# Moving the unfolding of the image rows from VectorE to GpSimd in a Fourier-space MLP

## What is computed

```python
xf = jnp.fft.rfft2(x, axes=(1, 2), norm='ortho')             # B, H, W//2+1, 8 blocks, 96
xr, xi = (xf.real, xf.imag)
o1r = relu(einsum(xr, w1[0]) - einsum(xi, w1[1]) + b1[0])    # 'bhwni,nio->bhwno'
o1i = relu(einsum(xi, w1[0]) + einsum(xr, w1[1]) + b1[1])
o2r = einsum(o1r, w2[0]) - einsum(o1i, w2[1]) + b2[0]
o2i = einsum(o1i, w2[0]) + einsum(o1r, w2[1]) + b2[1]
xc = softshrink(stack([o2r, o2i]), 0.01)                     # as complex numbers
out = jnp.fft.irfft2(xc, s=(H, W), axes=(1, 2), norm='ortho') + x
```

## Time and profile before

| | |
|---|---|
| median of 3 runs | 5438.11 us |
| profiled execution, own time | 5438.1 us |
| its span, first to last instruction | 5436.3 us |
| TensorE busy | 5260.5 us, 97% |
| VectorE busy | 3214.6 us, 59% |
| ScalarE busy | 3140.4 us, 58% |
| GpSimd busy | 1254.0 us, 23% |
| HBM traffic | 78 GB/s over the span |
| mean granted TensorE clock | 0.991 |

### The profile page before, as it was taken

The page is one execution under the profiler, slowest core; times in us unless marked ns, Lnnn a source line. Parts: engine busy times, 40 slices in busy tenths (PEclk is TensorE's granted clock), DMA queues, the critical chain, the costliest instruction groups (busy, mean ns, idle before and its releaser), DMA issues.

```text
span 5436.3 us, 112618 instructions
## 1 busy us (share of the span) xinstructions
PE 5260.5 (97%) x42112; PEld 4947.7 (91%) x42112; DVE 3214.6 (59%) x5330; ACT 3140.4 (58%) x5680; POOL 1254.0 (23%) x810
## 2 busy tenths in 40 slices
PE   8999999999999999999999999999999999999997
PEld 8999989899898989999999999998999999999997
DVE  4666556565565665656656566565665556655565
ACT  6555566555665556655566555665556655566554
POOL 2211222112222022220222202222022220222200
PEclk9999999999999999999999999999999999999999
DMA  3331233321333213332133321334313333123312
GB/s 106 98 97 43 59 99 98 98 48 52 99 98 99 51 49 98 98 99 58 42 98 98 99 66 44 88 98 99 84 40 75 98 99 90 41 68 98 99 48 47
DMA packets 1131613, 430.06 MB, mean 79 GB/s; under 512 B 1130784, under 2 KB 1130912, under 8 KB 1131040
## 3 DMA queue, kind: packets, MB, share of 16 engines
q1 hardware_dynamic: 1131040, 422.23, 31.0%
HBM read 220.82 MB, written 201.33 MB: 78 GB/s over the span
## 4 chain that ended last, share of the span: by engine, by line
PE 95%; issue 2%; DVE 2%; ACT 1%; DMA 0%; DVEq 0%; SPq 0%; ACTq 0%
PE psum L563 17%; PE psum L604 14%; PE psum L578 13%; PE psum L653 13%; PE psum L627 13%; PE psum L637 8%; PE psum L590 7%; PE psum L665 4%; PE psum L666 3%; PE psum L667 3%; DVE x L529 1%; DVE mixed L498 1%; PE psum L622 0%; PE psum L645 0%; PE psum L644 0%
## 5 line engine op out<-in xcount | busy, mean ns | idle before, releaser
L498 DVE COPY mixed<-psum 128x768 f32<-128x768 f32 (+1 forms) x544 | 508.2, 934 | 1356.0 <-PE psum L590 1356.0
L332 POOL TENSOR_TENSOR doubled<-x 128x768 f32<-128x768 f32 x248 | 358.9, 1447 | 3883.0 <-DMA x<-x 3862.9
L563 PE MATMUL psum<-mats,x 128*96 128x128 f32 x8192 | 930.1, 277 | 63.9 <-issue 47.3
L563 PEld LDWEIGHTS psum<-mats,x 128*96 128x96 f32 x8192 | 918.2, 166 | 73.9 <-issue 53.8
L434 ACT ACTIVATE sums_high<-psum 128x512 fp32r<-128x512 f32 x768 | 459.9, 599 | 775.8 <-PE psum L653 775.8
L604 PEld LDWEIGHTS psum<-mats,mixed 128*128 128x128 f32 x6272 | 744.0, 191 | 121.1 <-issue 112.0
L604 PE MATMUL psum<-mats,mixed 128*128 128x128 f32 x6272 | 841.8, 283 | 0.0
L653 PE MATMUL psum<-mats,spectrum 128*128 128x128 f32 x6144 | 814.7, 278 | 26.4 <-DVE spectrum L505 26.4
L578 PE MATMUL psum<-w_whole,whole 128*128 128x192 f32 x4160 | 779.4, 329 | 55.7 <-ACT whole L365 47.0
L653 PEld LDWEIGHTS psum<-mats,spectrum 128*128 128x128 f32 x6144 | 756.9, 194 | 31.1 <-DVE spectrum L505 31.1
L627 PE MATMUL psum<-w2t,hidden 128*128 128x192 f32 x4160 | 768.4, 327 | 0.0
(11 more groups left out here) (69 smaller groups left out, 6403.6 us busy)
## 6 DMA issues: line engine op xcount, KB each, us to landing
x<-x SPq DMA_DIRECT2D x160, 768.0 KB, 7.3
out<-x SPq DMA_DIRECT2D x160, 768.0 KB, 8.2
x<-x SPq DMA_DIRECT2D x32, 1488.0 KB, 9.6
out<-x SPq DMA_DIRECT2D x32, 1488.0 KB, 10.6
x<-x SPq DMA_DIRECT2D x32, 816.0 KB, 4.9
out<-x SPq DMA_DIRECT2D x32, 816.0 KB, 4.6
w2t<-L_conv_w SPq DMA_DIRECT2D x128, 36.0 KB
w_halved<-L_conv_w SPq DMA_DIRECT2D x128, 24.0 KB
```

The lines of the kernel that those rows point to most:

```text
L498: dve.tensor_copy(mixed[s % 2][:, 0:k], both_b(s)[:, 0:k]).then_inc(b_copied, 1)
L563: last = pe.matmul(bank_a(at)[:, i * SIZE:(i + 1) * SIZE], xs[par][:, slot, :], mat(FW_EVEN if slot <= HALF else FW_ODD), start=True, stop ...
```

## The change

GpSimd does the unfolding for every unit. The three additions of the fold go into a helper, `halves` (the first two of them), which fold and a new `unfold` share; `unfold` waits for `f_added`, then makes the same 8 steps of 8 rows, each with three instructions, and counts `unfolded` 8 times a unit in place of 4. The rows 0 and 64 are not touched in it. GpSimd's program becomes: fold unit 1; then for each unit: unfold it, wait for that, fold the next unit of the same buffer, wait for that; at the end unfold the last two units. VectorE's loop over `PIECES` and the semaphore `unfold_even` are gone, so that VectorE goes from L529 straight to L468. A store waits for two counts of `unfolded` a piece.

```diff
@@ SyncE, store @@
-                    sp.wait_ge(unfolded, (m * 2 + par) * NP + (i + 1))
+                    sp.wait_ge(unfolded, (m * 2 + par) * NFOLD + 2 * (i + 1))
@@ GpSimd @@
+            def halves(t, i, done):
+                lo, hi = i * FOLD_ROWS + 1, min((i + 1) * FOLD_ROWS, HALF - 1)
+                up, down, twice = t[:, lo:hi + 1, :], mirrored(t, lo, hi), doubled[:, 0:hi + 1 - lo]
+                pool.tensor_tensor(twice, down, down, ALU.add).then_inc(pool_steps, 1)
+                pool.tensor_tensor(up, up, down, ALU.add).then_inc(pool_steps, 1)
+                return down, up, twice
...
+            def unfold(m, par, steps):
+                n = m * 2 + par
+                pool.wait_ge(f_added, n * NF + NF)
+                for i in range(NFOLD):
+                    if i > 0:
+                        pool.wait_ge(unfolded, n * NFOLD + i)
+                    down, up, twice = halves(xs[par], i, unfolded)
+                    pool.wait_ge(pool_steps, steps + 2 * (i + 1))
+                    pool.tensor_tensor(down, up, twice, ALU.subtract).then_inc(unfolded, 1)
...
-            fold(0, 1)
-            with pool.Fori(1, PAIRS) as m:
+            fold(0, 1, 0)
+            pool.wait_ge(x_folded[1], NFOLD)
+            with pool.Fori(0, PAIRS - 1) as m:
                 for par in range(2):
-                    pool.wait_ge(x_folded[1 - par], (m + par) * NFOLD)
-                    fold(m, par)
+                    steps = (1 + (m * 2 + par) * 2) * (2 * NFOLD)
+                    unfold(m, par, steps)
+                    pool.wait_ge(unfolded, (m * 2 + par + 1) * NFOLD)
+                    fold(m + 1, par, steps + 2 * NFOLD)
+                    pool.wait_ge(x_folded[par], (m + 2) * NFOLD)
+            for par in range(2):
+                unfold(PAIRS - 1, par, (1 + (PAIRS - 1) * 4 + par) * (2 * NFOLD))
+                pool.wait_ge(unfolded, ((PAIRS - 1) * 2 + par + 1) * NFOLD)
@@ VectorE, at the end of a unit @@
-                    dve.wait_ge(f_added, n * NF + NF)
-                    for i in range(NP + 1):
-                        if i < NP:
-                            lo, hi = PIECES[i]
-                            dve.tensor_tensor(x_unit[:, lo:hi + 1, :], x_unit[:, lo:hi + 1, :], mirrored(x_unit, lo, hi),
-                                              ALU.add).then_inc(unfold_even, 1)
-                        if i > 0:
-                            lo, hi = PIECES[i - 1]
-                            dve.wait_ge(unfold_even, n * NP + i)
-                            dve.scalar_tensor_tensor(mirrored(x_unit, lo, hi), mirrored(x_unit, lo, hi), -2.0,
-                                                     x_unit[:, lo:hi + 1, :], op0=ALU.mult,
-                                                     op1=ALU.add).then_inc(unfolded, 1)
```

More of the change, by code:

```diff
@@ L229, in fourier_mlp @@
         pool_steps, dve_sums = sem("pool_steps"), sem("dve_sums")
-        unfold_even, unfolded = sem("unfold_even"), sem("unfolded")
+        unfolded = sem("unfolded")
         block = ctx.enter_context(nc.Block())
@@ L319, in _, with fold @@
         def _(pool):
-            def fold(m, par):
+            def halves(t, i, done):
[4 more added lines that the diff above has]
+                return down, up, twice
+            def fold(m, par, steps):
                 t = xs[par]
-                steps = (m * 2 + par - 1) * (2 * NFOLD)
                 for i in range(NFOLD):
-                    lo, hi = i * FOLD_ROWS + 1, min((i + 1) * FOLD_ROWS, HALF - 1)
                     if i % 2 == 0:
                         pool.wait_ge(x_loaded[par][i // 2], (m + 1) * (16 * len(ROWS[i // 2])))
-                    up, down, twice = t[:, lo:hi + 1, :], mirrored(t, lo, hi), doubled[:, 0:hi + 1 - lo]
                     if i > 0:
                         pool.wait_ge(x_folded[par], m * NFOLD + i)
-                    pool.tensor_tensor(twice, down, down, ALU.add).then_inc(pool_steps, 1)
-                    pool.tensor_tensor(up, up, down, ALU.add).then_inc(pool_steps, 1)
+                    down, up, twice = halves(t, i, x_folded[par])
                     ends = t[:, 0:1] if i == 0 else t[:, HALF:HALF + 1]
```

## The result

The changed kernel takes 5559.5 us (median of 4 runs, 5555.3 to 5563.2), the kernel before 5439.5 beside it: a ratio of 1.022 with an interval of 1.0202 to 1.0238, 120 us slower. The direction and the mechanism of the forecast held; its size, 5794, did not. It lies in the stated range only because that was drawn wide enough for two cases; the measured time fits neither of them.

What follows compares the result with a forecast made beforehand. TensorE, 95% of the chain, was taken to bound the kernel. To 5438.1 us were added 282 for waits on blocked copies, 53 for the clock and 20.5 at the program's end: 5793.6, with an 8-in-10 range of 5453 to 5900.

Steps and rivals of the forecast that it cites:

- What bounds the kernel: TensorE is 95% of the chain that ended last; other engines' work costs only if TensorE waits or after its last matmul.
- what is removed: Eight VectorE unfolding instructions a unit, 13.7 us, lying beside stage A; removing them gains 0 in 31 of 32 units.
- Blocking: VectorE's double-rate copies inside SBUF wait for GpSimd's instructions; TensorE's L590 waits 9.1 us a passage; chance 0.56 with alternation.
- the price of a turn: Each VectorE copy beside GpSimd's stream costs its own 0.23 us and one GpSimd instruction of 1.70 us, so 1.93.
- strict alternation: When both wait, GpSimd's next instruction goes before VectorE's next one, so each copy waits for a whole GpSimd instruction.
- My sum for this term: TensorE's L590 waiting for the copies in 31 passages of 9.1 us each: 282 us.
- The clock: Each of 31 TensorE stalls loses 1.7 us at the lower clock level: 53 us.
- The end: After the last matmul nothing covers GpSimd's last unfolding of 41.0 us and the last piece's transfer: +20.5 us.
- The round trip: The buffer's stores, loads, weights and fold come 17 to 22 us later, under a 58 us cover: costs nothing.
- free: Rival: copies aren't held up, or only the first of a run; only the program's end costs, 5458.6 us; chance 0.33.
- Blocked longer: Rival: VectorE gets in only where GpSimd waits for its semaphore, or after the stream; 423 us of waits, 5935; chance 0.06.
- not slower: Rival: the loop edge's half-speed stretch goes, 20.4 us come back and meet the end's 20.5; 5438 us; chance 0.05.

Runs made afterwards that it cites:

- later: Changed kernel with GpSimd unfolding each unit, except the last, only after VectorE's L511 and L512 of the next unit: 5465.8 us, ratio 1.0040.
- shorter: Changed kernel with the unfolding in GpSimd instructions of 4 rows in place of 8, 48 instead of 24 a unit: 5467.1 us, ratio 1.0043.
- at single rate: Changed kernel with the ten copies L505 to L512 made as reductions over an axis of length 1: 5465.2 us, ratio 1.0037.
- added alone: Kernel before, VectorE still unfolding, plus 24 idle GpSimd additions behind f_added of each of the first 30 units: 5910.3 us, ratio 1.0868.
- the three that take the turns away: Changed kernel with unfolding behind the copies (5465.8 us), with GpSimd instructions of half the length (5467.1 us), or with the copies as reductions (5465.2 us).
- both costs are taken away: Changed kernel with GpSimd unfolding behind L511 and L512 of the next unit and VectorE unfolding the last unit: 5445.6 us, ratio 1.0011.

## Why the prediction was right and wrong

- **What bounds the kernel, what is removed**: right. Taking the unfolding from VectorE gained nothing; with it left out altogether the kernel is where it was.
- **Blocking**: right, and shown by four kinds of runs: later, shorter, at single rate, and added alone. The reason that I chose this bound (that it is the double-rate instructions that now fall beside GpSimd) fits the run with reductions. It was half of the matter: L536, single-rate by my own reading of 1.14 ns an element, waits as well when GpSimd streams beside it. The page "SBUF — State Buffer" of the Trainium skill, section "Who interferes with whom", says the same of which instructions contend, two-input ones included, and the trace agrees (1698 ns for 204, 2938 for 1751).
- **The step that failed** is the price of a turn: "each costs its own 0.23 us and one GpSimd instruction", 1.93 us, ten times. Measured: 12.4 us for ten in place of 18.5. It has two parts. A copy's own time does not add to the turn: it ends 0.1 us behind the end of a GpSimd instruction, and GpSimd's next one is not held up by it. A step of three takes 5.28 us beside the copies and 5.2 without them (from 2089.26 to 2094.44 in the same trace). I had added 0.23 for each copy to both sides. And the strict alternation that I assumed does not hold: three of ten copies wait for no turn, because they stand behind a copy that waited, read from the same partition as it, and GpSimd waits for a semaphore there. Seven GpSimd instructions with their gaps, from 2281.68 to 2294.05, are 12.4 us. My last sentence named this step as the weak one: if a run of copies gets through behind one wait, the time goes towards 5459.
- **How that became a factor of three.** TensorE's wait is what is left of the copies' time behind a cover of fixed length. I forecast 9.1 us a passage; measured, L596 starts 3.1 us late within a pair (0.8 before L584, 2.3 behind it), and over all 31 passages the mean is 2.4. Copies of 18.5 against 12.4 us, a third less, turn into 9.1 against 3.1. My sum for this term was 282 us; the waits grew by 74.
- **The clock**: 53 us forecast for the stalls, 25 to 30 measured in all. In a stretch at clock 0.50 I take half of its length as lost. Added up over the traces: behind the stalls at the start of B 36 us, but these stretches stand behind 14 of the 31 only, and five of them are two or four times as long as the others. At the loop's edge it is 29 us, where it was 20. At the start of E nine stretches, 15 us, are gone, for idle times of the same 1.65 us; no run shows why. Which stalls have a stretch behind them can't be had from their length alone.
- **The end**: 20.5 forecast, 19.3 measured in the profile. The unfolding took 40.9 us (from 5509.2, when L549 ends, to 5550.2; forecast 41.0), and 7.2 us followed (forecast 8.2).
- **The round trip**: right that it costs nothing. The fold began 56 us behind the end of F (forecast 60), TensorE never waited for it:

```profile
2128.91 1.61 POOL L353 TENSOR_TENSOR x<-x,doubled 128x672 f32<-128x672 f32 x1
2145.04 1.47 POOL L324 TENSOR_TENSOR doubled<-x 128x768 f32<-128x768 f32 x1 [14.52 <-DMA x<-x]
```

- **The rivals**: free (5459) was wrong for this kernel and came out within about 3 us for the three that take the turns away (5465 to 5467, beside a kernel before that was itself 5 us higher). Blocked longer and not slower did not come. The row on which the latter rests, 3.19 us of idle time with a half-speed stretch and 3.02 without, does not sort all edges of the kernel before: the three without a stretch stand behind 2.99, 3.00 and 3.02 us, but two of the twelve with one behind 2.97 and 2.98. What none of my cases had was blocking with some copies let through; I had it at all or nothing, and gave the space between 5470 and 5706 no chance.
- **Left open**: some 6 us that stay when both costs are taken away, 3 of which are TensorE's longer idle time at the loop's edge; and why a copy gets through in its neighbour's turn only where GpSimd waits for a semaphore.

## What to carry to other kernels

Before work is moved to GpSimd, list which VectorE instructions will fall beside it: those that copy inside SBUF at double rate, and those with two inputs in SBUF, then wait for whole GpSimd instructions, and one long stream can hold up a handful of tiny copies on which TensorE hangs. Where they can't be kept apart, cutting GpSimd's instructions in half, placing its stream behind the copies, or copying with a single-rate reduction each took away the whole stall here. And where a wait is a long chain minus a fixed cover, an error of a third in the chain is one of three times in the wait: price it as a range, not as a product.

## What the runs showed of the hardware that I had not expected

- The waiting is part of the instruction's recorded length (204 ns become 1698), with no idle time before it. A list of waits doesn't show it; the mean by shape does.
- A short VectorE instruction takes next to nothing from GpSimd (a mean of 1828 ns for L353 in the changed kernel, 1814 where no copy runs beside it), a long one with two inputs does (1467 to 1936).
- A copy can go in the turn of the copy before it. It has to read from the same first partition (one tiny instruction between them, reading elsewhere, costs it the turn: 81 of 93 against none, 5567 against 5648 us), the one before has to have waited itself, and GpSimd has to wait for a semaphore at that point (246 of 247 against none of 114).
- The Trainium skill, page "VectorE: DVE Perf Modes", section "Two Vector instructions with no wait between them", names a change of the first quadrant (32 partitions), of the input or of the output, as what makes an instruction wait until all before it have finished. The traces agree in when instructions start. With the value read from partition 0, the copy behind the reduction starts 0.07 us before the reduction ends (2273.58 and 2273.65); with partition 64 it starts behind its end (2305.91 and 2305.90). The reduction itself reads from partition 0 as the copy before it does and writes elsewhere, and starts behind that one's end (2273.51 and 2273.49). But such a start is not a lost turn: the two copies into `halved` write from partitions 0 and 64, the second starts behind the first's end (2286.90 and 2286.89 in the changed kernel), and they share a turn. Only the change of the input goes with the loss.
